# A six-sublayer decoder on one core: another table of turns for its two lanes, with the same instructions

## Chip, cores and metric

The kernel runs on one core of a Trainium2 chip. The metric is the device time of one execution in microseconds (us); the time of a kernel is the median of its runs. TensorE (PE) multiplies matrices, VectorE (DVE), ScalarE (ACT) and GpSimd (POOL) work on elements, and SyncE (SP) issues most of the transfers.

## The reference

Input x is 4 sequences of 512 tokens with 128 channels, and there is a context of 32 tokens for each sequence. Six sublayers follow each other, each as `x = layernorm(x + f(x))`:

```python
x = ln(x + mamba(x))                 # selective scan over 512 tokens, 256 channels, 16 states
x = ln(x + cross_attention(x, ctx))  # 16 heads of 64, inner layernorm, gate
x = ln(x + experts(x))               # shared FFN and 8 experts of 512, top 2 of 8
x = ln(x + window_attention(x))      # 16 heads of 8, causal window of 128, rotary
x = ln(x + cross_attention(x, ctx))  # 16 heads of 8
x = ln(x + two_local_layers(x))      # 8 heads of 64, window 64, then a gated FFN of 341, twice
```

All of it is float32 in the interface, and every sequence goes through all six in order.

## The kernel before

The four sequences go over the core in two lanes. Lane 0 takes sequences 0 and 1, one after the other, lane 1 takes 2 and 3; I call a lane's first sequence pass 1 and its second pass 2. Each lane has buffers of its own (names ending in `_0` and `_1`) and four of the eight PSUM banks, so the two lanes never share data. They do share the engines, and one engine executes its instructions strictly in program order, waits included. An instruction of lane 1 that must wait therefore holds back whatever of lane 0 stands behind it on that engine, and the other way round.

Each stage is written once for each engine, as a Python generator that yields at the places where the engine may be handed over (`mamba_vector`, `cross_tensor` and so on). For each engine `interleave` then merges the two lanes by the table `TURNS`: the first number says how many steps lane 0 takes, the next how many lane 1 takes, and so on in turn.

```python
lanes, done = (first, second), object()
for lane in lanes:
    next(lane)
last = [next(lanes[k % 2], done) for k, n in enumerate(turns) for _ in range(n)]
```

There is one list each for PE, ACT, DVE, POOL and SP. So the table alone decides the order of the instructions of one lane against those of the other on each engine. Within a lane the order is that of the generators.

The stages and the lines that the text below names:

- **Setup**, run once, in lane 1 ahead of its first stage. PE folds the context into the weights of the two cross attentions (L563, L567, L575, L584, L592, L597), DVE takes the results out of PSUM (L517, L524, L536, L538) and makes a rotary table (L552).
- **Mamba.** A preamble (projections L702, L706, L712, L719 and L726 on PE; the convolution L855 and L857 on DVE; the step size, L789 to L805 on ACT and L865 to L882 on DVE) and then the scan over 16 states. Each state takes on DVE one product L893 and two scans L901, on ACT two decays L822 and a copy L829, on POOL one product L930, on PE two broadcasts L738 and two sums L749. The decay of a lane lies in one PSUM bank: ACT writes it, the scan reads it, and only then can the next decay be written. After the 16th state come L907 (gating), L760 on PE, the residual L676 and two layernorms (L628 to L640).
- **Cross attention**: four tiles of 128 tokens. For each, PE L956, DVE L1023 and L1024, ACT L989, DVE L1014 and L1015, POOL L1038, PE L970, ACT L995, PE L962. Then the residual L678 and a layernorm (L609 to L618, with the root L652 on POOL).
- **Experts.** The shared FFN (PE L1064, L1094), routing on DVE (L1178 to L1241), a scatter of the tokens to DRAM by POOL, and then 15 blocks of 128 sorted tokens. L1105 transposes the sorted tokens, L1119 is the up and L1133 the down product of a block. The weights of a block are 512 KB, loaded by SP (L1921) into a ring of four buffers for each lane. Then a gather by POOL (L1286) and a layernorm.
- **Window attention**: PE L1459, L1466, L1441, then 14 units with PE L1325, L1330 (scores), DVE L1422, ACT L1385 and PE L1312.
- **Second cross attention and two local layers**: PE L1552, L1597 to L1629, ACT L1717, DVE L1771 to L1847, and the gated FFN (statistics PE L1640 and L1643, ACT L1735 and L1738, DVE L1842 to L1847; products PE L1650 and L1653, ACT L1744, DVE L1857; PE L1657 and L1665, DVE L1862).

Of the kernel before, what the change touches and what calls it, by code (L numbers as in the profile page):

```python
# [103 lines left out]
        4, 4, 1, 21, 2, 1, 1, 1, 1, 2, 1, 5, 1, 1, 1, 2, 3, 2, 3, 4, 3, 1, 5, 1, 1, 2, 2, 2, 1, 3, 3, 3, 3, 3,  # L104
        2, 1, 2, 2, 1, 3, 3, 3, 3, 5, 3, 3, 3, 3, 3, 3, 2, 3, 1, 3, 1, 5, 1, 1, 3, 1, 6, 1, 2, 4, 1, 1, 4, 3, 1,
        2, 2, 6, 1, 2, 3, 1, 4, 1, 4, 9, 2, 2, 14, 4, 2, 1, 1, 1, 1, 1, 5, 2, 2, 3, 2, 2, 4, 3, 1, 14, 1, 1, 1,
        1, 1, 1, 23, 1, 5, 1, 3, 1, 1, 2, 1, 1, 1, 1, 1, 1, 1, 4, 1, 1, 1, 5, 2, 2, 2, 1, 1, 1, 4, 1, 4, 3, 2,
        1, 1, 1, 2, 3, 3, 2, 3, 1, 1, 5, 5, 4, 2, 1, 3, 4, 1, 2, 2, 3, 2, 1, 1, 1, 1, 5, 3, 2, 1, 3, 3, 1, 2, 1,
        1, 3, 1, 2, 2, 3, 1, 1, 1, 1, 3, 6, 1, 5, 1, 4, 1, 3, 2, 2, 1, 2, 1, 1, 1, 1, 1, 1, 6, 1, 2, 3, 3, 2, 1,
        8, 1, 1, 1, 1, 3, 2, 1, 1, 1, 1, 6, 1, 1, 7, 7, 2, 2, 1, 1, 2, 3, 3, 1, 3, 1, 2, 2, 2, 4, 4, 7, 4, 1, 3,  # L110
        1, 2, 1, 2, 3, 4, 6, 4, 2, 2, 2, 1, 1, 3, 1, 2, 2, 4, 1, 2, 1, 3, 3, 1, 4, 3, 3, 2, 1, 2, 4, 1, 3, 3, 2,
        2, 3, 5, 8, 3, 1, 2, 5, 3, 1, 2, 1, 1, 2, 2, 3, 2, 2, 4, 6, 4, 1, 1, 1, 4, 2, 2, 4, 4, 4, 4, 2, 1, 2, 2,
        1, 3, 1, 2, 2, 4, 1, 2, 1, 3, 3, 1, 4, 3, 3, 7, 5, 5, 4, 2, 1, 3, 5, 2, 3, 3, 3, 3, 4, 3, 2, 1, 3, 2, 1,
        3, 7, 3, 3, 3, 4, 4, 2, 1, 2, 1, 1, 2, 2, 1, 1, 2, 3, 3, 2, 3, 1, 3, 1, 5, 1, 1, 3, 1, 6, 1, 1, 2, 1, 1,
        1, 2, 4, 3, 2, 1, 1, 7, 1, 2, 3, 1, 4, 1, 1, 1, 2, 2, 1, 6, 1, 2, 15, 3, 2, 2, 2, 1, 3, 1, 2, 1, 2, 3,
        1, 1, 1, 2, 4, 1, 1, 16, 1, 2, 1, 1, 22, 1, 2, 1, 1, 1, 3, 2, 1, 1, 2, 4, 1, 2, 1, 2, 1, 1, 1, 3, 2, 4,
        2, 1, 1, 2, 1, 2, 2, 1, 4, 3, 3, 2, 2, 1, 1, 3, 3, 1, 1, 2, 1, 1, 1, 2, 3, 2, 2, 3, 5, 2, 1, 2, 4, 1, 1,
# [2048 lines left out]
```

## Time and profile before

| | before |
|---|---|
| Median of 3 runs | 1492.87 us (1489.36 to 1494.64) |
| Time of the profiled execution | 1502.43 us |
| Its span, from the first to the last instruction | 1500.6 us |
| PE, DVE, ACT, POOL busy | 81%, 66%, 54%, 26% of the span |
| Mean granted clock of TensorE | 0.91 of full speed |

The profile is of one execution, which took 9.6 us longer than the median of the runs. "Busy" is the time in which an engine executed an instruction; "idle before" is how long it stood still ahead of one. A granted clock of 1.00 is 2.4 GHz and one of 0.50 is 1.2 GHz; numbers between are means over a stretch.

### The profile page before, as it was taken

Reading aid. Unit: us, or ns where it says so; the run is one execution under the profiler, and the core shown is the slowest. Engines: PE = TensorE matmul, PEld = TensorE weight load, DVE = VectorE, ACT = ScalarE, POOL = GpSimd, SP = SyncE. Lnnn points to the kernel's source line nnn. Section 1 sums busy time; section 2 is a strip of 40 time slices with the busy share of each in tenths; the row PEclk is TensorE's granted clock in tenths of the full one; section 3 lists DMA queues with packets and bytes.
Section 4 is the critical chain, followed back from the end, with each engine's and each line's share of the span. In section 5 each row is a group of like instructions: output and inputs, shape, how many; then the busy total and the mean of one; then the engine's idle time right before and its main releaser. Section 6 shows DMA issues by size and latency. Waiting matters only on the chain.

```text
span 1500.6 us, 23083 instructions
## 1 busy us (share of the span) xinstructions
PE 1210.9 (81%) x8416; PEld 773.4 (52%) x8416; DVE 988.3 (66%) x1914; ACT 813.1 (54%) x2170; POOL 393.6 (26%) x248
## 2 busy tenths in 40 slices
PE   5668768897799789889875776788879987888986
PEld 4313235786566446556531232468846654565563
DVE  5789976414555689459559999651265556984974
ACT  2365523263576367757637643225447734776873
POOL 0045732603000143023011666242220013311310
PEclk9878988899799999999987998779989988999998
DMA  8300000675000011001010000037710000000100
GB/s 304 129 0 1 0 1 0 197 251 158 6 2 2 1 43 30 1 8 30 7 28 0 1 0 1 0 115 238 226 34 1 2 1 8 22 16 8 29 9 15
DMA packets 42177, 72.20 MB, mean 48 GB/s; under 512 B 3793, under 2 KB 27473, under 8 KB 41810
## 3 DMA queue, kind: packets, MB, share of 16 engines
q1 hardware_dynamic: 40018, 66.53, 14.0%
q0 software_dynamic: 2048, 4.20, 0.9%
q8 instruction: 68, 1.11, 0.3%
q14 instruction: 43, 0.35, 0.1%
HBM read 51.19 MB, written 13.24 MB: 43 GB/s over the span
## 4 chain that ended last, share of the span: by engine, by line
PE 48%; DVE 25%; ACT 14%; issue 7%; DMA 3%; POOL 2%; SPq 0%; DVEq 0%; POOLq 0%; ACTq 0%
DVE scratch L901 5%; PE psum L1330 4%; PE psum L1552 3%; PE psum L1119 3%; DVE scratch L893 3%; PE psum L1312 3%; ACT scratch L1717 3%; ACT scratch L1385 3%; PE psum L749 3%; PE psum L1133 2%; PE psum L1441 2%; PE psum L1325 2%; PE psum L956 2%; PE psum L1597 2%; PE psum L1627 2%
## 5 line engine op out<-in xcount | busy, mean ns | idle before, releaser
L930 POOL TENSOR_TENSOR scratch<-scratch 128x1024 f32<-128x1024 f32 x64 | 151.9, 2384 | 141.0 <-DVE scratch L901 122.0
L652 POOL TENSOR_TENSOR small<-small,w_const 128x16 f32<-128x16 f32 x32 | 95.5, 2990 | 254.1 <-DVE small L1761 254.1
L901 DVE TENSOR_TENSOR_SCAN scratch<-psum,scratch 128x512 f32<-128x512 f32 x128 | 149.8, 1206 | 8.6 <-ACT psum L822 7.9
L749 PE MATMUL psum<-scratch,w_const 128*128 128x512 f32 x256 | 141.1, 681 | 14.6 <-POOL scratch L930 14.6
L652 POOL TENSOR_TENSOR rstd<-rstd,w_const 128x4 f32<-128x4 f32 x32 | 32.5, 1019 | 387.0 <-DVE rstd L614 379.2
L1385 ACT ACTIVATE scratch<-psum,mx 128x256 f32<-128x256 f32 (+1 forms) x256 | 111.1, 457 | 26.2 <-DVE mx L1422 25.5
L822 ACT ACTIVATE psum<-scratch,a_neg 128x512 f32<-128x512 f32 x128 | 88.0, 691 | 60.9 <-DVE scratch L901 58.7
L738 PE MATMUL psum<-scratch,cb 96*128 96x512 bf16 x128 | 50.8, 422 | 73.9 <-DVE scratch L893 65.7
L1422 DVE TENSOR_REDUCE mx<-psum 128x4 f32<-128x1024 f32 (+1 forms) x56 | 68.2, 1220 | 51.8 <-PE psum L1330 51.8
L1171 ACT ACTIVATE scratch<-psum,scratch 128x128 f32<-128x128 f32 x240 | 68.2, 372 | 60.5 <-PE psum L1119 60.5
L1552 PE MATMUL psum<-w_local,hT 128*128 128x512 f32 x192 | 96.0, 628 | 1.7 <-ACT hT L1534 1.7
L1717 ACT ACTIVATE scratch<-psum,mx 128x128 f32<-128x128 f32 x256 | 91.2, 404 | 10.6 <-DVE mx L1808 10.5
L1251 DVE COPY scratch<-psum 128x128 f32<-128x128 f32 x60 | 16.7, 289 | 116.8 <-PE psum L1133 116.7
L749 PEld LDWEIGHTS psum<-scratch,w_const 128*128 128x128 f32 x256 | 51.4, 214 | 68.6 <-issue 41.2
L1119 PE MATMUL psum<-scratch,expert_weights 128*128 128x128 f32 x480 | 67.6, 287 | 16.3 <-DMA expert_weights<-in_expert_weights 11.7
L738 PEld LDWEIGHTS psum<-scratch,cb 96*128 96x128 bf16 x128 | 13.0, 102 | 129.7 <-DVE scratch L893 96.6
L893 DVE TENSOR_TENSOR scratch<-scratch,psum 128x1024 f32<-128x1024 f32 x64 | 75.9, 1200 | 6.0 <-PE psum L738 5.7
L1312 PE MATMUL psum<-w_const,scratch 128*128 128x128 f32 x448 | 69.5, 292 | 5.2 <-ACT scratch L1371 3.3
L1119 PEld LDWEIGHTS psum<-scratch,expert_weights 128*128 128x128 f32 x480 | 60.6, 199 | 20.7 <-DMA expert_weights<-in_expert_weights 14.8
L829 ACT ACTIVATE scratch<-psum 128x512 f32<-128x512 f32 x64 | 38.0, 594 | 55.6 <-PE psum L738 55.5
L1330 PE MATMUL psum<-scratch 32*128 32x256 f32 (+1 forms) x512 | 67.6, 390 | 0.0
L1312 PEld LDWEIGHTS psum<-w_const,scratch 128*128 128x128 f32 x448 | 52.2, 148 | 27.8 <-issue 23.2
(274 smaller groups left out, 3060.0 us busy)
## 6 DMA issues: line engine op xcount, KB each, us to landing
expert_weights<-in_expert_weights SPq DMA_DIRECT2D x61, 512.0 KB, 4.8
scratch<-scratch SPq DMA_DIRECT2D x48, 128.0 KB, 2.3
folded_products<-expert_weights SPq DMA_DIRECT2D x8, 512.0 KB, 2.6
folded<-folded_products SPq DMA_DIRECT2D x8, 512.0 KB, 3.8
w_local<-in_local SPq DMA_DIRECT2D x1, 3122.0 KB
sorted_y<-scratch SPq DMA_DIRECT2D x12, 256.0 KB, 5.3
scratch<-sorted_x SPq DMA_DIRECT2D x4, 704.0 KB, 6.6
scratch<-in_cross SPq DMA_DIRECT2D x1, 2624.5 KB, 12.7
```

Of the source, the lines that this page charges most:

```text
L652: t.eng.tensor_tensor(v, v, W("const", "neg_half").to_broadcast([P, v.shape[1]]), ALU.pow).then_inc(t.s[done], 1)
L749: ins = pe.matmul(sum_banks[c], ident, t.m.hC[:, 2 * ((n - 1) % 2) + c, :], start=(n == 1), stop=(n == NS))
L822: act.activation(t.ps["dA"], t.m.delta[:, c, :], ACT.Exp, scale=a_neg[:, c, n:n + 1])\
L893: dve.tensor_tensor(t.m.dBu[n % 2], t.m.du[:, :, :], bank, ALU.mult).then_inc(t.s["v_freed"], 1)
L901: dve.tensor_tensor_scan(t.m.hs[:, n % 2, c, :], t.ps["dA"], t.m.dBu[n % 2][:, c, :], 0.0, ALU.mult, ALU.add)\
L930: t.eng.tensor_tensor(t.m.hC[:, 2 * (n % 2):2 * (n % 2) + 2, :], t.m.hs[:, n % 2], C, ALU.mult)\
L1119: ins = pe.matmul(tok(bank, f), t.m.weights[b % BUFS][:, f * P:(f + 1) * P], tok(t.m.xsT, b), start=(f == 0), stop=(f == NF - 1), skip_gro ...
L1312: ins = pe.transpose(tok(bank, c), tok(t.m.wide_pr[:, n % 2, u, :], c), ident)
L1330: ins = pe.matmul(banks[u][:, a * nk * P:(a + 1) * nk * P], t.m.wide_qT[r:r + 32, g, j * P:(j + 1) * P], t.m.wide_kT[r:r + 32, g, (j + 1 - ...
L1385: ins = act.activation(t.m.wide_pr[:, n % 2, u, z], bank[:, z], ACT.Exp, bias=t.m.mx2[:, c:c + 1], accum_out=t.m.sums[:, j % 2, h:h + 1])
L1552: pe.matmul(ring.open(), tok(t.m.hT, i), w_qkv[:, c * 512:(c + 1) * 512], start=True, stop=True).then_inc(t.s[sig], 1)
L1717: ins = act.activation(tok(t.m.pr[:, u, :], a), tok(bank, a), ACT.Exp, bias=t.m.mx2[:, c:c + 1], accum_out=t.m.sums2[:, c:c + 1])
```

## The change

Each of the five lists of `TURNS` is replaced by another. Nothing else differs: no generator, no buffer, no semaphore and no shape. Of the 76 lines of the table one stands here as it was and as it is, the start of PE's list; the numbers themselves say little to a reader.

```diff
     "pe": [
-        4, 4, 1, 21, 2, 1, 1, 1, 1, 2, 1, 5, 1, 1, 1, 2, 3, 2, 3, 4, 3, 1, 5, 1, 1, 2, 2, 2, 1, 3, 3, 3, 3, 3,
+        5, 9, 4, 7, 1, 10, 2, 3, 1, 1, 2, 2, 1, 1, 2, 1, 7, 1, 2, 3, 1, 1, 5, 2, 4, 2, 3, 1, 4, 1, 2, 1, 1, 3,
```

The new table is a line longer, so every line number of the code is one higher in the changed kernel (L712 becomes L713). What the lists do is seen in the order of the built programs. On DVE, ACT, PE, POOL and SP each lane executes the same instructions in the same order as before, and only their merging differs. ACT has one more kind of instruction that follows from the order: where two neighbours need functions from different tables, the compiler puts a table load between them. There are 45 of these in the program before and 51 after. Four of the added ones are in the first mamba, two in the first experts stage of lane 0 (around an exponential of lane 1's cross attention), one at the end of pass 1, and at the end of pass 2 there is one less.

PE near the start, before: lane 0's preamble (scratch_0, w_mamba) against the setup (scratch_1, expert_weights).

```order
L567 MATMUL psum<-scratch_1 128x128 x2
L575 MATMUL psum<-scratch_1 128x64 x8
L584 MATMUL psum<-scratch_1 64x128 x8
L575 MATMUL psum<-scratch_1 128x64 x8
L584 MATMUL psum<-scratch_1 64x128 x8
L575 MATMUL psum<-scratch_1 128x64 x8
L584 MATMUL psum<-scratch_1 64x128 x8
L575 MATMUL psum<-scratch_1 128x64 x8
L712 MATMUL psum<-scratch_0,w_mamba 8x512 x2
L719 MATMUL psum<-scratch_0,w_mamba 96x512 x2
```

The same place after:

```order
L703 MATMUL psum<-xT_0,w_mamba 128x512 x2
L707 MATMUL psum<-xT_0,w_mamba 128x512 x2
L564 MATMUL psum<-scratch_1 128x128 x9
L713 MATMUL psum<-scratch_0,w_mamba 8x512 x2
L720 MATMUL psum<-scratch_0,w_mamba 96x512 x2
L727 MATMUL psum<-scratch_0,w_mamba 128x512 x2
L564 MATMUL psum<-scratch_1 128x128 x7
L739 MATMUL psum<-scratch_0,cb 128x512
L568 MATMUL psum<-scratch_1 128x128 x2
L576 MATMUL psum<-scratch_1 128x64 x8
```

Lane 0's preamble stood behind seven groups of L575 and L584 and now stands ahead of all of them. DVE is alike: the last pair of L857 of lane 0 stood behind 16 of L517 and all 8 of L524, and stands behind one of L517 now; before lane 0's first L893 stood all of the setup, and 4 of the 16 instructions L536 and L538 stand there now. Lane 1's first stage starts on DVE (L844) after the first scan product of lane 0 before, and after six states of lane 0 now.

DVE where lane 1 ends its first mamba, before (y_0, mx_0 and sums_0 are lane 0, in its cross attention):

```order
L893 TENSOR_TENSOR scratch_1<-scratch_1,psum 128x1024
L633 TENSOR_SCALAR rstd2_0<-mv_0 128x4
L635 TENSOR_SCALAR rstd_0<-mv_0 128x4
L901 SCALAR_TENSOR_TENSOR scratch_1<-psum,scratch_1 128x512 x2
L640 TENSOR_SCALAR scratch_0<-y_0,mv_0,rstd2_0 128x128 x4
L640 TENSOR_SCALAR x_0<-y_0,mv_0,rstd_0 128x128 x4
L1023 TENSOR_REDUCE mx_0<-psum 128x16
L907 TENSOR_TENSOR scratch_1<-psum,scratch_1 128x512 x2
```

The same place after:

```order
L894 TENSOR_TENSOR scratch_1<-scratch_1,psum 128x1024
L902 SCALAR_TENSOR_TENSOR scratch_1<-psum,scratch_1 128x512
L679 TENSOR_TENSOR y_0<-psum,x_0 128x512
L902 SCALAR_TENSOR_TENSOR scratch_1<-psum,scratch_1 128x512
L610 BN_STATS rowstat_0<-y_0 128x6 x4
L613 BN_AGGR mv_0<-rowstat_0 128x2 x4
L615 TENSOR_SCALAR rstd_0<-mv_0 128x4
L619 TENSOR_SCALAR x_0<-y_0,mv_0,rstd_0 128x128 x4
L908 TENSOR_TENSOR scratch_1<-psum,scratch_1 128x512 x2
```

The end of lane 1's mamba stood next to the start of lane 0's cross attention and now stands behind its end: lane 0 leads by a stage more. In the experts stage this lead is given back. Before lane 1's first transpose of sorted tokens (L1105) PE had 6 blocks of lane 0 finished before and has 8 now, and after it follow 24 blocks of both lanes before and 22 now. Lane 0's window attention, which started on PE ahead of lane 1's last two blocks, starts behind them all. From the second cross attention of pass 1 on, the two orders are close to each other, within a few instructions at most places.

PE at the very end of pass 2, before (the gated FFN of both lanes):

```order
L1569 MATMUL psum<-w_local,scratch_1 128x128 x4
L1650 MATMUL psum<-scratch_0,w_local 128x512
L1653 MATMUL psum<-scratch_0,w_local 128x512
L1650 MATMUL psum<-scratch_0,w_local 128x512
L663 MATMUL psum<-w_const,x_1 128x128 x4
L1653 MATMUL psum<-scratch_0,w_local 128x512
L1650 MATMUL psum<-scratch_0,w_local 85x512
L1640 MATMUL psum<-hT_1,w_const 128x512
L1653 MATMUL psum<-scratch_0,w_local 85x512
L1657 MATMUL psum<-w_rows 128x512
L1643 MATMUL psum<-scratch_1,w_const 128x512
L1665 MATMUL psum<-w_local,scratch_0 128x128 x12
```

The same place after:

```order
L1570 MATMUL psum<-w_local,scratch_1 128x128 x4
L1644 MATMUL psum<-scratch_0,w_const 128x512
L664 MATMUL psum<-w_const,x_1 128x128 x4
L1641 MATMUL psum<-hT_1,w_const 128x512
L1644 MATMUL psum<-scratch_1,w_const 128x512
L1651 MATMUL psum<-scratch_0,w_local 128x512
L1654 MATMUL psum<-scratch_0,w_local 128x512
L1651 MATMUL psum<-scratch_0,w_local 128x512
L1651 MATMUL psum<-scratch_1,w_local 128x512
L1654 MATMUL psum<-scratch_1,w_local 128x512
L1651 MATMUL psum<-scratch_1,w_local 128x512
L1654 MATMUL psum<-scratch_0,w_local 128x512
```

Lane 1's last transpose and statistics moved ahead of all of lane 0's gated products, and the two lanes' products alternate. At the end of pass 1 the move is another: there lane 0's twelve L1665 stood behind lane 1's first three gated products, and stand ahead of them now, and on ACT lane 0's last L1744 stood behind lane 1's L1738 and stands ahead of it.

## Rows read from the trace of the kernel before

**Rows 1.** Busy time of the engines, clock by slice, chain that ended last (page).

```profile
PE 1210.9 (81%) x8416; PEld 773.4 (52%) x8416; DVE 988.3 (66%) x1914; ACT 813.1 (54%) x2170; POOL 393.6 (26%) x248
...
PEclk9878988899799999999987998779989988999998
...
PE 48%; DVE 25%; ACT 14%; issue 7%; DMA 3%; POOL 2%; SPq 0%; DVEq 0%; POOLq 0%; ACTq 0%
```

**Rows 2.** Stretches: window, length, busy of PE PEld DVE ACT POOL, PEclk, DMA share, GB/s.

```profile
62.80:190.80 128.00, 94.15 (x203) 33.94 (x203) 116.35 (x113) 73.67 (x112) 71.03 (x31) 0.86 0.02 7
...
305.00:366.00 61.00, 51.38 (x410) 48.18 (x408) 13.00 (x62) 29.50 (x100) 8.78 (x9) 0.94 0.65 210
366.00:386.00 20.00, 13.07 (x81) 8.90 (x81) 12.74 (x47) 8.71 (x26) 8.84 (x9) 0.84 0.23 64
386.00:414.00 28.00, 24.62 (x154) 15.55 (x153) 14.44 (x53) 15.20 (x53) 0.00 (x0) 0.81 0.00 1
414.00:500.00 86.00, 76.85 (x828) 50.76 (x826) 50.32 (x84) 58.59 (x224) 1.01 (x1) 1.00 0.01 2
```

**Rows 3.** Timeline of the start: start us, us, engine, line, [idle before <-releaser].

```profile
23.32 4.85 DVE L517 TENSOR_TENSOR scratch<-psum,w_const 128x256 f32<-128x256 f32 x13
28.17 4.87 DVE L524 TENSOR_TENSOR expert_weights<-psum,w_const 128x512 f32<-128x512 f32 x8
...
34.98 1.34 ACT L789 ACTIVATE scratch<-scratch,w_mamba 128x512 f32<-128x512 f32 x2 [13.61 <-DVE scratch L857]
...
39.02 1.88 PE L712 MATMUL psum<-scratch,w_mamba 128*8 128x512 f32 x4
...
58.68 2.76 DVE L552 TENSOR_TENSOR tab<-scratch 128x256 f32<-128x256 f32 x8
...
62.80 1.22 DVE L893 TENSOR_TENSOR scratch<-scratch,psum 128x1024 f32<-128x1024 f32 x1
```

**Rows 4.** Timeline of DVE: both L907, lane 0's L618 and lane 1's L1233.

```profile
190.77 1.26 DVE L907 TENSOR_TENSOR scratch<-psum,scratch 128x512 f32<-128x512 f32 x2
...
215.01 1.28 DVE L907 TENSOR_TENSOR scratch<-psum,scratch 128x512 f32<-128x512 f32 x2
...
245.07 1.11 DVE L618 TENSOR_SCALAR x<-y,mv,rstd 128x128 f32<-128x128 f32 x4
...
281.42 0.17 DVE L1233 TENSOR_SCALAR scratch<-scratch 128x15 uint32<-128x15 f32 x1
```

**Rows 5.** The records of L1133 alone, 8 for a block; columns as in rows 2.

```profile
305.00:366.00 61.00, 25.37 (x194) 23.17 (x192) 0.94 0.65 210
```

**Rows 6.** Timeline of PE: lane 1's first L1105, lane 0's last L1133, both window starts (L663).

```profile
304.98 0.60 PE L1105 MATMUL psum<-w_const,scratch 128*128 128x128 f32 x4
...
336.51 2.05 PE L1133 MATMUL psum<-expert_weights,scratch 128*128 128x128 f32 x16 [0.54 <-ACT scratch L1171]
...
358.71 1.12 PE L663 MATMUL psum<-w_const,x 128*128 128x128 f32 x4 [2.22 <-DVE x L618]
...
385.58 1.06 PE L663 MATMUL psum<-w_const,x 128*128 128x128 f32 x4
```

**Rows 7.** Timeline of ACT and PE at the end of pass 1.

```profile
753.15 0.63 ACT L1738 ACTIVATE scratch<-scratch 128x512 f32<-128x512 f32 x1
753.80 1.28 ACT L1744 ACT_TABLE_LOAD   x1
755.09 0.68 ACT L1744 ACTIVATE scratch<-psum,w_local 85x512 f32<-85x512 f32 x1
...
759.51 2.84 PE L1665 MATMUL psum<-w_local,scratch 128*128 128x128 f32 x24
```

**Rows 8.** Timeline of PE at the end of pass 2.

```profile
1469.72 0.60 PE L663 MATMUL psum<-w_const,x 128*128 128x128 f32 x4
...
1475.69 2.84 PE L1665 MATMUL psum<-w_local,scratch 128*128 128x128 f32 x24
1480.36 1.12 PE L1650 MATMUL psum<-scratch,w_local 128*128 128x512 f32 x2 [1.82 <-DVE scratch L1847]
```

131 rows, old and new, of the table TURNS are left out of this document.

## Prediction

> **What bounds the kernel now.** I began with the busy times. PE is busy for 81% of the span, and 48% of the chain that ended last are PE's, 25% DVE's, 14% ACT's [rows 1]. No engine is the bound throughout, so I went on by stretches of time. In 62.8 to 190.8, the first mamba, DVE is busy for 116.35 of 128 us, 91%, and PE for 94.15, at a clock of 0.86: DVE bounds. In 305 to 366, the expert blocks of both lanes, PE has 51.38 of 61. In 366 to 386, where lane 0 starts its window and lane 1 waits for its gather, no engine reaches 14 of 20 us, and the 28 us behind it, with PE at 24.62, run at a clock of 0.81. From 414 to 500 PE has 76.85 of 86 at a clock of 1.00 [rows 2]. A table of turns takes no work away. It can gain only where the bounding engine stands idle (1.0 − 0.91 of the mamba, some 20 us of PE between 305 and 414: 9.6 + 6.9 + 3.4), where PE's clock is low, and at the start, at the pass boundary and at the end, where one lane is alone.
>
> **The start.** The engines obey program order, so I looked in the timeline for work of the setup ahead of lane 0's preamble. ACT's L789 at 34.98 waited 13.61 us for a result of DVE L857, and this L857 stood behind thirteen L517 (4.85 us) and eight L524 (4.87). PE's L712 follows at 39.02 [rows 3]. With both groups behind it L857 ends 9.7 us earlier; the two or three L536 and L538 that also stood ahead of it are some 0.6 more. So L789 comes at about 24.7. From L789 to lane 0's first L893 at 62.80 are 27.8 us. In that piece DVE now also has the 9.7 us of L517 and L524, but no longer twelve of L536 and L538 (about 0.65 each, 7.8), the eight L552 (2.76 [rows 3]) and 1.3 us of small ones, together 11.9. 27.8 + 9.7 − 11.9 = 25.6, and the first L893 comes at 24.7 + 25.6 = 50.3, 12.5 us earlier.
>
> **Lane 0's mamba and cross attention.** Between lane 0's first L893 and its L907 stand, by the order of instructions, 11.9 us of setup more and six L893 and twelve L901 of lane 1 fewer, at 1.2 us each (the L893 of [rows 3] took 1.22): 21.6 less. 116.35 + 11.9 − 21.6 = 106.6 us of DVE work, at the density of now, 0.909, take 117.3. Lane 0's L907 comes at 50.3 + 117.3 = 167.6 instead of 190.77 [rows 4], 23 earlier. Here I chose the old density; six states of lane 0 alone could be less dense, with nothing of the other lane to fill the wait from scan to decay. L907 to the last L618 of lane 0's cross attention took 54.3 us (245.07 − 190.77 [rows 4]), which gives 221.9.
>
> **Lane 1.** What was moved ahead of it is its price. Its L907 stood next to lane 0's first L1023 and stands behind lane 0's L618 now: about 223.5 instead of 215.01, 8.5 later. From there to the end of its routing, L1233 at 281.42, were 66.4 us [rows 4]; less of lane 0 stands in that way, which I put at 4 us, an estimate from the few cross instructions of 0.7 to 1.3 us that are no longer there. L1233 comes at about 286, and the first L1105, 23.6 us later as now (304.98 − 281.42, [rows 4, 6]), at 309.5, 4.5 later. Queued behind that L1105 on PE are all further blocks of lane 0. They would wait with it.
>
> **The expert blocks.** 194 records of L1133 in 61 us [rows 5] are 24 blocks, 2.54 us each. After lane 1's first L1105 there are 22 blocks now, since two more of lane 0 stand ahead of it: 309.5 + 22 × 2.54 = 365.4, against 366. The 4.5 us are paid for. Lane 1's window start, at 385.58 [rows 6], hangs on its last block and stays within 1 us. Lane 0's last L1133 was at 336.51 and its window's first transpose 22.2 later, at 358.71 [rows 6]. Now this L663 stands behind lane 1's blocks, at 366 to 367. In the old order PE had blocks to do until 366 anyway, so most of these 8 us are no loss. I put the stretch up to 500 at +2, with −8 and +10 as bounds. The −8 would need the stretch of 28 us to lose its idle 3.4 us and its low clock (0.19 of 24.62 is 4.7). The +10 is what remains if lane 0's window is late by 8 us with nothing in its place, and 2 us at low clock.
>
> **From 500 on.** The orders differ by few instructions until the end of pass 1. There lane 0's last L1744 (755.09) stood behind a table load of 1.28 and an L1738 of 0.63 of lane 1, and its L1665 at 759.51 behind lane 1's gated products [rows 7]. Lane 0 begins pass 2 with what L1665 gives: −2, between 0 (DVE has lane 1's statistics to do in the meantime) and −4. At the end of pass 2, PE's transpose L663 of lane 1 at 1469.72 stood behind lane 0's gated products, and PE idled 1.82 us before lane 1's L1650 at 1480.36, behind the 24 L1665 of lane 0 [rows 8]. With L663 ahead of all products it comes some 3 us earlier, and products of lane 0 fill the wait: −4, between 0 and −6.
>
> **Table loads.** Six more on ACT, each 1.28 us; the activation behind one starts 0.01 us after its end (753.80 + 1.28, 755.09 [rows 7]). ACT is busy 73.67 of 128 us in the mamba, and 29.50 of 61 with the experts [rows 2]. I put them at 0, since DVE's and PE's work hides them; without this cover, they are 7.7 us. The Trainium skill (ScalarE: Activation LUTs, What ACT_TABLE_LOAD costs) gives about 2.66 us for every switch, as it adds a drain to the load, by which six would be 16 us. The rows here show no such drain.
>
> **The sum.** +2 − 2 − 4 + 0 = −4 us, against the profiled execution (1502.43 us, 9.6 above the median), so 1498.4 for it and 1489 on the scale of the median, 1492.87. All that lane 0 gains in the first 220 us is given back in the experts stage, as the merged order makes the lanes meet there.
>
> **The rivals.** A difference below 0.3%, 4.5 us, can't be told from none here.
>
> *The lead is kept (1478).* Lane 0's blocks begin earlier, its weights arrive while lane 1 is still in its routing, and both lanes' blocks and windows fit into PE's gaps. Between 305 and 414 lie 19.9 us of idle PE and 4.7 of low clock [rows 2]; half of them, 11, come off besides my 4. For it speaks that the blocks take 2.54 us each where PE works 2.14 (51.38 / 24), against it that the DMA engines are busy for 0.65 of that time, and that lane 1 is behind.
>
> *Nothing changes (1493).* The first 23 us vanish and the ends are held by DVE, whose last statistics follow one another whatever PE does. For it speaks that DVE is next to PE in each end.
>
> *Lane 1 starves PE (1505).* Lane 1's L907 is tied to lane 0's L618. If scanning lane 0 alone is less dense, or its cross attention has waits of its own, and L618 comes at 234.5 instead of 222, L907 is at 236, 21 later than before, and lane 1's first L1105 at 322. PE stands before it with lane 0's blocks queued behind. That is 12.5 us of wait beyond my sum, and then a run at a low clock: 8 us at 0.5 instead of 0.94 lose 3.5. −4 + 12.5 + 3.5 = +12. It decides the sign from where L618 is later than about 227 (5 us of wait and 3.5 of clock against the 4). In this kernel the clock was 0.86 where PE was busy 74% and 1.00 where it was busy 89% [rows 2]. By the Trainium skill (TensorE: Matmul & The Clock Gate, Part 1: The HAM clock gate) idle gaps bring the half clock back, so such a wait is paid for twice; the rows agree in direction.
>
> *Table loads on the path (1497).* Six loads of 1.28 us come off the ACT chain between scan and decay and before lane 0's expert activations: −4 + 7.7 = +4.
>
> **How the numbers follow.** The forecast has 0.42, of which 0.18 lie beyond −4.5; its own range is 1484 to 1494. The lead is kept 0.22, nothing changes 0.08, PE starves 0.20, table loads 0.08, half of that slower than the bound. Faster 0.18 + 0.22 = 0.40, within 0.24 + 0.08 + 0.04 = 0.36, slower 0.20 + 0.04 = 0.24. The range reaches from a little below the kept lead, 1476, to just over the starved case, 1506.
>
> **What the profile would show.** L789 near 25 and lane 0's first L893 near 50; lane 0's L907 near 168 and L618 near 222, lane 1's L907 right behind it; L1105 of lane 1 near 310 with little idle time ahead of it; the last block near 366, lane 1's window start near 385; the same stages as now from 500 on, less 2 us after 760 and 4 at the end. The prediction is wrong if PE idles for more than some us before lane 1's L1105 (slower), if the last block comes before 358 (the lead is kept), or if the second pass, which I hold for nearly unchanged, drifts by more than 3 us.

## The result, and the profile after

| | before | changed |
|---|---|---|
| Median, first chip | 1493.76 us (4 runs, 1489.36 to 1505.45) | 1473.69 us (4 runs, 1467.91 to 1480.25) |
| Ratio, first chip | | 0.9876 (95% interval 0.9841 to 0.9911) |
| Profiled execution: span, mean clock | 1500.6 us, 0.91 | 1478.5 us, 0.915 |

The change makes the kernel 1.24% faster, 18.5 us by the ratio and 20 by the two medians. I had forecast 4 us, inside the bound of what a measurement tells from none, and the measured time lies below my range. Two later timings of the changed kernel gave 0.9859 and 0.9865. The ratios leave out executions more than 1.5% above the fastest of the same kernel: four of the twelve of e5_start, and one of the kernel before.

Busy times, clock by slice and the chain that ended last, of the changed kernel's page (before: [rows 1]):

```profile
PE 1204.4 (81%) x8416; PEld 771.2 (52%) x8416; DVE 983.9 (67%) x1914; ACT 818.2 (55%) x2176; POOL 393.3 (27%) x248
...
PEclk9678999998799989999987999889979989999998
...
PE 46%; DVE 25%; ACT 15%; issue 7%; POOL 3%; DMA 3%; SPq 0%; DVEq 0%; POOLq 0%; ACTq 0%
```

Nothing in these sums says where 20 us went. The work is the same, and ACT has its six table loads more. The start and the front of the changed kernel, from its timeline (start us, us, engine, line; lines are one higher than before):

```profile
24.12 1.33 ACT L790 ACTIVATE scratch<-scratch,w_mamba 128x512 f32<-128x512 f32 x2 [2.69 <-DVE scratch L858]
25.89 1.88 PE L713 MATMUL psum<-scratch,w_mamba 128*8 128x512 f32 x4
47.95 1.21 DVE L894 TENSOR_TENSOR scratch<-scratch,psum 128x1024 f32<-128x1024 f32 x1
179.34 1.26 DVE L908 TENSOR_TENSOR scratch<-psum,scratch 128x512 f32<-128x512 f32 x2
230.66 1.12 DVE L619 TENSOR_SCALAR x<-y,mv,rstd 128x128 f32<-128x128 f32 x4 [1.12 <-POOL rstd L653]
231.69 1.28 DVE L908 TENSOR_TENSOR scratch<-psum,scratch 128x512 f32<-128x512 f32 x2
288.36 0.18 DVE L1234 TENSOR_SCALAR scratch<-scratch 128x15 uint32<-128x15 f32 x1
307.47 0.60 PE L1106 MATMUL psum<-w_const,scratch 128*128 128x128 f32 x4
351.31 1.16 PE L1134 MATMUL psum<-expert_weights,scratch 128*128 128x128 f32 x8 [0.40 <-ACT scratch L1172]
355.56 1.12 PE L664 MATMUL psum<-w_const,x 128*128 128x128 f32 x4 [3.09 <-DVE x L619]
378.40 1.11 PE L664 MATMUL psum<-w_const,x 128*128 128x128 f32 x4
```

Against [rows 3, 4, 6]: L789 comes at 24.12 instead of 34.98 and the first L893 at 47.95 instead of 62.80, both as worked out. Lane 0's L907 is at 179.34, 12 us later than my 167.6, and yet the last block of the experts is done at 352.5 and not at 365. The same kernel's stretches (window, length, busy of PE, PEld, DVE, ACT, POOL, clock, DMA share, GB/s), to be held against [rows 2]:

```profile
48.00:179.30 131.30, 99.51 (x265) 44.74 (x265) 111.82 (x119) 66.77 (x103) 56.20 (x25) 0.79 0.09 36
307.80:354.00 46.20, 40.28 (x350) 39.17 (x348) 9.73 (x39) 25.61 (x88) 8.30 (x9) 1.00 0.76 228
354.00:384.00 30.00, 20.12 (x82) 13.19 (x82) 15.37 (x82) 9.47 (x26) 9.10 (x10) 0.62 0.15 42
384.00:414.00 30.00, 27.04 (x193) 17.33 (x194) 16.01 (x39) 18.86 (x80) 0.00 (x0) 0.87 0.00 1
```

The blocks are denser and finished sooner; the hole between blocks and windows, 30 us with PE at 20.12 and a clock of 0.62, is as large as before or larger, and only earlier. DVE in the first mamba is busy for 0.85 of the stretch in this execution, whose clock was low at the start, not for the 0.91 that I had carried over.

### The profile page after: what moved, and what is told of

Read it like the earlier page. It is cut to its first block, busy times and chain, and to the rows that moved or that the text cites. A ratio compares the mean times of both kernels' runs of the same rounds, so it can differ in the third digit from the quotient of the medians.

```text
span 1478.5 us, 23087 instructions
## 1 busy us (share of the span) xinstructions
PE 1204.4 (81%) x8416; PEld 771.2 (52%) x8416; DVE 983.9 (67%) x1914; ACT 818.2 (55%) x2176; POOL 393.3 (27%) x248
## 4 chain that ended last, share of the span: by engine, by line
PE 46%; DVE 25%; ACT 15%; issue 7%; POOL 3%; DMA 3%; SPq 0%; DVEq 0%; POOLq 0%; ACTq 0%
DVE scratch L902 6%; PE psum L1331 3%; ACT scratch L1718 3%; PE psum L1553 3%; DVE scratch L894 3%; ACT scratch L1386 3%; PE psum L1313 2%; PE psum L1120 2%; PE psum L1134 2%; PE psum L750 2%; PE psum L957 2%; PE psum L1326 2%; PE psum L1442 2%; PE psum L1349 1%; PE psum L664 1%
## 5 line engine op out<-in xcount | busy, mean ns | idle before, releaser
L1553 PE MATMUL psum<-w_local,hT 128*128 128x512 f32 x192 | 92.3, 611 | 1.6 <-ACT hT L1535 1.3
L739 PEld LDWEIGHTS psum<-scratch,cb 96*128 96x128 bf16 x128 | 13.3, 104 | 123.5 <-DVE scratch L894 88.1
L1134 PE MATMUL psum<-expert_weights,scratch 128*128 128x128 f32 x480 | 64.1, 280 | 0.8 <-ACT scratch L1172 0.4
```

Source lines behind the costliest of these rows:

```text
L1134: ins = pe.matmul(bank[:, 0:D], t.m.hid[:, k % 2, f, :], t.m.weights[k % BUFS][:, FF + f * P:FF + (f + 1) * P], start=(f == 0), stop=(f == ...
L1553: pe.matmul(ring.open(), tok(t.m.hT, i), w_qkv[:, c * 512:(c + 1) * 512], start=True, stop=True).then_inc(t.s[sig], 1)
```

## The experiments

Both tables run through common states: points at which on every engine both have executed the same steps of both lanes. At such a point one table can be followed by the other. I used five: at about 350 us (end of the expert blocks of pass 1), 500 us (end of its window), 770 us (pass boundary) and 975 us (end of the cross attention of pass 2), and for one run 550 us. A run with such a joined table changes the order in its stretch and nowhere else, and keeps the line numbers of before. All ratios are against the kernel before, timed in the same session on the same chip, since chips differ: the kernel before had medians of 1510.86, 1497.38, 1495.16 and 1495.04 us in the four sessions, of which the second and the fourth were on one chip.

### Which stretch holds the gain: e1_front, e2_locals, e3_second

The edits, each as one piece of the difference in order against before. e1_front, PE at the start (as in the changed kernel up to 500 us):

```diff
-L706 MATMUL psum<-xT,w_mamba 128x512
-L563 MATMUL psum<-scratch 128x128 x4
-L706 MATMUL psum<-xT,w_mamba 128x512
-L563 MATMUL psum<-scratch 128x128 x12
+L706 MATMUL psum<-xT,w_mamba 128x512 x2
+L563 MATMUL psum<-scratch 128x128 x9
+L712 MATMUL psum<-scratch,w_mamba 8x512 x2
```

e2_locals, PE behind the join at 500 us (one piece of many):

```diff
-L970 MATMUL psum<-w_const,scratch 128x128 x4
+L1552 MATMUL psum<-w_local,hT 128x512 x3
+L970 MATMUL psum<-w_const,scratch 128x128 x4
+L962 MATMUL psum<-folded,scratch 128x128 x4
```

e3_second, PE in the cross attention of pass 2, where the last sums L749 of lane 1's scan stood ahead of lane 0's scores L956:

```diff
-L749 MATMUL psum<-scratch,w_const 128x512 x2
 L951 MATMUL psum<-w_rows 128x512
 L956 MATMUL psum<-folded,xT 128x512
+L749 MATMUL psum<-scratch,w_const 128x512 x2
+L956 MATMUL psum<-folded,xT 128x512
```

> The new table up to the end of pass 1's window attention, the old one behind it. In the two profiles lane 1 ends this window at 515 before and 513 after, lane 0 at 494 and 498. Theory A (the gain comes mostly from the second pass, where the two tables differ only by swaps of 1 to 4 neighbours): this run gains 2 us, between 0 and 5, so 1491 on the scale where before is 1493, and the second half of its profile looks like before's. Theory B (the second pass only inherits an arrangement of the lanes from the first 500 us): this run has most of the 20 us, 1473 to 1480.

> The old table, but the new one from the second cross attention of pass 1 to the end of pass 1 (500 to 770 us). In the profiles lane 0 leaves this stretch 7.9 us earlier and lane 1 4.5 us earlier, of which 2 were there before it. Theory A: 3 to 6 us faster, and the second pass as long as before. Theory B, now with the pass boundary as the place that arranges the lanes: the 3 us of lead that lane 0 gains at the boundary make the scan of pass 2 denser, so 10 to 14 us faster. My prediction had -2 for this stretch.

> The old table up to the pass boundary at 770 us, the new one for all of pass 2. Theory A: 13 to 16 us faster, of which about 8 in the mamba, 4 in the cross attention, 3 in the experts and 2 to 4 in the last stage. Theory B: the same instructions with neighbours swapped are worth nothing, and only the end's 2 to 4 us are gained. My prediction had -4 for this stretch.

| run | ratio (95%) | in us |
|---|---|---|
| e1_front | 0.9932 (0.9904 to 0.9960) | −10.3 |
| e2_locals | 0.9987 (0.9961 to 1.0014) | −2.0, not told from none |
| e3_second | 0.9969 (0.9942 to 0.9995) | −4.7 |

The us are (1 − ratio) × 1510.86. Neither theory holds as it was put. The front has about half of the gain and not the 2 us that I had read from the two profiles, nor all of it. The second pass has about a quarter. The 12 to 15 us which the first pair of profiles showed in pass 2 were mostly the two executions and not the order.

### Do the stretches add up: a2_changed, a3_changed

The changed kernel itself (its diff is the change), in two more sessions on one chip.

> The changed kernel again, on the chip of the next three. The first 500 us alone gave 0.68%, the locals 0.13% and the second pass 0.31%, 1.12% together. Theory A (the stretches add up): 1.0 to 1.3% faster. Theory B (they help each other, since a lead won in one is used in the next): more than 1.4%. For the start: in the first profile of the changed kernel TensorE's clock was 0.50 from 34 to 64 us and lane 0's L907 came at 179.3; the same order in the run of the front had it at 1.00, and L907 at 170.6. If the clock there is chance, this profile has either.

> The changed kernel again on the same chip, to compare the run of this call with, and for the state of the clock at the start: 0.94 to 1.00 in 34 to 64 us goes with L907 of lane 0 at 170 to 173, 0.50 with 179 to 181. The time is 1.2 to 1.5% below before.

0.9859 (0.9836 to 0.9882) and 0.9865 (0.9840 to 0.9890). The three stretches give 0.68 + 0.13 + 0.31 = 1.12%; within the intervals they add up, and a gain of the stretches from each other is not shown. Nor is it excluded: 1.41% is at the edge of theory B.

### Where in the front: e6_to_experts, e5_start, e7_old_start

e6_to_experts follows the new table up to the end of the expert blocks at 350 us and the old one behind it. Up to there its edit is that of e1_front, of which this is another piece, on PE: lane 1's preamble (L712, L719, L726) stands among later states of lane 0, between more of its L738 and L749. Behind the join lane 0's L663 stands ahead of lane 1's last blocks, as before.

```diff
 L712 MATMUL psum<-scratch,w_mamba 8x512 x2
 L719 MATMUL psum<-scratch,w_mamba 96x512 x2
+L738 MATMUL psum<-scratch,cb 128x512
+L744 MATMUL psum<-scratch,w_const 128x512 x2
+L749 MATMUL psum<-scratch,w_const 128x512 x2
 L726 MATMUL psum<-scratch,w_mamba 128x512 x2
```

> The new table up to the end of the expert blocks of pass 1 (about 350 us), the old one behind it. Theory A (the lead of lane 0 pays in the experts stage, because its blocks start earlier and lane 1's last block comes 8 to 10 us earlier than before): 8 to 10 us faster, as with the whole front (0.68%). Theory B (the gain needs the new order of the window too, where lane 0's L663 is behind lane 1's blocks): less than 5 us faster. Both have lane 1's last L1133 at 348 to 352, since the order up to there is the same.

0.9934 (0.9907 to 0.9960), −9.9 us: the time of theory A. The new order of the window stage adds nothing that these intervals show; the gain is made before 350 us. But its reason failed, and so did what both theories had: lane 1's last L1133 ended at 359.9, not at 348 to 352, with two of its blocks behind the window start of lane 0 again. From lane 1's first L1105 to its last block (columns as in [rows 2]):

```profile
307.00:360.00 53.00, 44.24 (x366) 42.99 (x365) 12.00 (x58) 26.34 (x89) 8.67 (x9) 0.94 0.65 199
```

These are 53 us, where the first profile of the changed kernel has 45 (307.47 to 352.47), and the gain is that of e1_front all the same. So how early the last block ends does not by itself set the time. Lane 1's window start, its L663, comes at 380.7 here, and at 378.40 and 379.9 in the two profiles of the changed kernel with the same low clock at the start.

e5_start moves the preamble only. All of the setup is still ahead of lane 0's first L893 (DVE):

```diff
-L517 TENSOR_TENSOR scratch<-psum,w_const 128x4x64 x13
-L524 TENSOR_TENSOR expert_weights<-psum,w_const 128x512 x8
-L538 COPY expert_weights<-psum 128x512
+L517 TENSOR_TENSOR scratch<-psum,w_const 128x4x64
 L857 SCALAR_TENSOR_TENSOR scratch<-psum,w_mamba,scratch 128x509 x2
```

> The old table, but the start as in the changed kernel: lane 0's mamba preamble ahead of the setup (L712 behind no L575 or L584, the last L857 behind one L517), with all of the setup still ahead of lane 0's first L893, and lane 1 never later than before. If the preamble behind the setup is a cost by itself, lane 0's first L893 comes 4 to 8 us earlier than 62.8 (DVE was busy for only 39.08 of these 62.8 us), both lanes keep it and the kernel is 4 to 8 us faster. If the start is given back whatever follows (lane 1's own preamble or the experts' weights set the time), the first L893 is earlier and the end within 2 us of before.

1.0015 (0.9988 to 1.0042), and its executions are spread widely, from 1503.62 to 1535.65 us. Both readings had the first L893 earlier, and in the profiled execution it came later. From its timeline:

```profile
71.87 1.20 DVE L893 TENSOR_TENSOR scratch<-scratch,psum 128x1024 f32<-128x1024 f32 x1
```

71.87 against 62.80 [rows 3]. The setup, pushed behind the preamble, ran on PE at half clock in this execution (29.46 of 30 us busy from 34 to 64 us, at 0.54), and the scan stood behind it. Its four pairs of L575 and L584 took 22.0 us, 5.5 each; a pair takes 3.0 in a2_changed at full clock. An estimate from these: at full clock the first L893 would have come 10 us earlier, at about 62, as before. So moving the preamble ahead is no gain by itself. The new table also puts the setup behind the first states; a run with that move alone was not made.

e7_old_start is the counterpart: the setup as before, all ahead of the first L893, then lane 0 alone for its first states, then the new order (DVE, against before):

```diff
 L893 TENSOR_TENSOR scratch<-scratch,psum 128x1024
+L901 SCALAR_TENSOR_TENSOR scratch<-psum,scratch 128x512 x2
+L893 TENSOR_TENSOR scratch<-scratch,psum 128x1024
+L901 SCALAR_TENSOR_TENSOR scratch<-psum,scratch 128x512 x2
```

> The new table, but all of the setup ahead of lane 0's first L893 as in the old one; then lane 0 alone for its first states, then the new order. It takes the start's 12 us away and keeps the distance between the lanes. If the start is worth what it brings (L893 at 48 instead of 62), this run is 8 to 12 us slower than the changed kernel, so about as fast as before. If the distance of the lanes is what matters and the start by itself is worth little, as the run with the start alone says (1.0015), it stays within 4 us of the changed kernel, 0.8% faster than before or more.

0.9929 (0.9905 to 0.9953), with a2_changed at 0.9859 on the same chip: 0.70%, 10.5 us slower than the changed kernel, as the first reading says, though not "about as fast as before". In the new order the start is worth what it brings. The other 0.7% remain, of which 0.44 are the stretches behind 500 us (e2_locals, e3_second), so about 0.3%, 4 us, are left for the distance of the lanes alone, which these intervals do not tell from none.

### The second pass: e4_mamba2, e8_late

e4_mamba2 has the new order only from 770 to 975 us. One piece on DVE, where lane 1's L907 let lane 0's cross attention wait:

```diff
 L1023 TENSOR_REDUCE mx<-psum 128x16
+L1024 TENSOR_TENSOR scratch<-psum,mx 128x512
 L907 TENSOR_TENSOR scratch<-psum,scratch 128x512 x2
-L1024 TENSOR_TENSOR scratch<-psum,mx 128x512
```

e8_late has it only behind 975 us. A piece of it on PE, in the window of pass 2, where lane 1's first transpose stands one unit of lane 0 earlier:

```diff
 L1330 MATMUL psum<-scratch 128x128 x8
+L663 MATMUL psum<-w_const,x 128x128 x4
 L1325 MATMUL psum<-cb 128x512 x2
 L1330 MATMUL psum<-scratch 128x128 x8
-L663 MATMUL psum<-w_const,x 128x128 x4
```

> The old table, with the new one only in the mamba and the cross attention of pass 2. In the first two profiles this piece (775 to 990 us) was 12 us shorter with the new table. Theory A (the swaps of neighbours in the scan matter): 4 to 8 us faster, the whole gain of the run with the new second pass (0.31%). Theory B (the 12 us were the clock of those two executions, 0.85 against 0.90): within 2 us of before, and the 0.31% come from the end.

> The old table up to the end of the cross attention of pass 2, the new one for the experts, the window and the last stages of pass 2. The run with only the mamba and the cross attention of pass 2 gave 0.22% (interval 0.5 to -0.1), the whole second pass 0.31%. Theory A (both halves of the second pass count; the experts of lane 1 took 111 to 115 us with the new order and 118 with the old one on two of the three chips): 3 to 6 us faster. Theory B (only the mamba and the cross attention count): within 2 us of before. My prediction had -4 for the end alone.

e4_mamba2: 0.9978 (0.9948 to 1.0008), −3.3 us, not told from none. e8_late: 0.9974 (0.9951 to 0.9996), −3.9 us. Each is near the 4.7 us (0.8 to 8.8) of the whole pass, and the three intervals overlap; how the gain splits stays open. DVE's longest waits in the last part of mamba and cross attention of pass 2, first in the kernel before (937 to 990 us), then in a2_changed (921 to 968), show one thing that moved:

```profile
DVE mx L1023 <- PE psum L956: 9.3, 4, 5.2
DVE sums L1014 <- ACT scratch L989: 3.1, 5, 0.7
```

```profile
DVE mx L1024 <- PE psum L957: 4.2, 3, 2.4
DVE sums L1015 <- ACT scratch L990: 1.9, 3, 0.7
```

The columns are us in total, times, longest. These two profiles differ by 5.1 us in the first of these waits. But over all profiles (880 to 1010 us) it goes with the order: the six with the old order in this piece have 6.7 to 9.3 us, the nine with the new one 4.2 to 6.0. Where the front is the old one too, 6.7 (e2_locals) and 9.3 stand against 6.0 and 6.0 (e3_second, e4_mamba2); where it is the new one, 7.2 and 7.7 (e6_to_experts, e1_front) against 4.2 to 4.5. So about 3 us of the wait go with the order, which fits the 3.3 us of e4_mamba2.

The end is settled by the traces as well. Lane 1's L1786 is a place up to which DVE has done the same work in both orders (kernel before, then changed):

```profile
1403.46 1.21 DVE L1786 TENSOR_TENSOR scratch<-scratch,small 128x1024 f32<-128x1024 f32 x1
```

```profile
1381.03 1.21 DVE L1787 TENSOR_TENSOR scratch<-scratch,small 128x1024 f32<-128x1024 f32 x1
```

From there to the end of the span are 97.2 us before (1500.6 − 1403.46) and 97.4 changed (1478.5 − 1381.03). In the other profiles it is 97.2 with the old order (98.4 in e6_to_experts) and 97.4 with the new one (97.8 in e3_second). The new order of the gated FFN at the end of pass 2 gains nothing; what e8_late gains lies between 975 us and this place.

### The clock at the start

Six profiles have the start of the changed kernel word for word. From 34 to 64 us, a2_changed and then e6_to_experts:

```profile
34.00:64.00 30.00, 27.01 (x185) 19.85 (x186) 29.94 (x42) 12.08 (x15) 4.72 (x2) 0.94 0.23 93
```

```profile
34.00:64.00 30.00, 29.31 (x149) 24.56 (x148) 22.86 (x32) 7.52 (x9) 2.37 (x1) 0.50 0.16 66
```

| profile | clock 34 to 64 us | lane 0's L907 |
|---|---|---|
| a2_changed | 0.94 | 172.4 |
| e1_front | 1.00 | 170.6 |
| f3_old_window | 1.00 | 171.3 |
| changed, first | 0.50 | 179.3 |
| e6_to_experts | 0.50 | 179.0 |
| a3_changed | 0.52 | 181.1 |

It is one or the other, and at the low level (1.2 GHz) L907 comes about 8 us later. It shows in the time: the three profiled executions with the low level took 4.3 to 6.6 us more than the median of their kernel's runs, the three others 0.6 to 3.3 less. PE is busy nearly all the time in it, 29.31 of 30 us. In the 20 us ahead of it, 14 to 34 us, PE was busy for 17.00 us at a clock of 0.99 in the first profile and for 16.07 us at 0.91 in a2_changed. In both the clock then fell at about 34 us. In a2_changed it was 0.57 from 34 to 38 us, with PE busy for 4.00 of 4 us, and 1.00 from 38 on; in the first profile it stayed at 0.50, with PE busy for 23.31 of 24 us from 36 to 60. So idleness ahead of it does not tell the two apart. By the Trainium skill (TensorE: Matmul & The Clock Gate, Part 1: The HAM clock gate) idleness is what brings the half clock; the trace agrees for the idle time of f5_scan_first below, and not for this fall. In the profiles of the old start the clock is 0.80 to 0.91 in the same 30 us. Two kernels tried to take the scan out of the way of this.

f2_broadcast, PE, against the new table:

```diff
 L575 MATMUL psum<-scratch 128x64 x8
 L584 MATMUL psum<-scratch 64x128 x8
+L738 MATMUL psum<-scratch,cb 128x512
 L575 MATMUL psum<-scratch 128x64 x8
 L584 MATMUL psum<-scratch 64x128 x8
 L575 MATMUL psum<-scratch 128x64 x8
 L584 MATMUL psum<-scratch 64x128 x8
-L738 MATMUL psum<-scratch,cb 128x512 x2
+L738 MATMUL psum<-scratch,cb 128x512
```

f5_scan_first has both L738 there, and on DVE, against the new table:

```diff
 L893 TENSOR_TENSOR scratch<-scratch,psum 128x1024
+L901 SCALAR_TENSOR_TENSOR scratch<-psum,scratch 128x512 x2
+L893 TENSOR_TENSOR scratch<-scratch,psum 128x1024
 L538 COPY expert_weights<-psum 128x512
-L901 SCALAR_TENSOR_TENSOR scratch<-psum,scratch 128x512
 L536 TENSOR_SCALAR expert_weights<-psum,gate 128x512
 L538 COPY expert_weights<-psum 128x512
-L901 SCALAR_TENSOR_TENSOR scratch<-psum,scratch 128x512
-L893 TENSOR_TENSOR scratch<-scratch,psum 128x1024
```

> The new table, with PE's broadcast L738 of lane 0's second half state moved ahead of the last two of the four pairs of groups L575 and L584. Where the clock is 0.50 from 34 to 64 us (three of five profiles with this start) each pair of groups takes 5.6 us on PE and DVE waits for this broadcast; two pairs are 11 us. Theory A (the low clock costs because the scan is queued behind the setup on PE): up to 8 us off at the low clock, none at the full clock, so 3 to 5 us faster than the changed kernel in the median and L907 of lane 0 near 171 at either clock. Theory B (the setup's copies on DVE are the limit at the low clock): L907 stays near 179 at the low clock and the time is the changed kernel's.

> The new table with two edits at the start. PE: the second and third broadcast L738 of lane 0 stand behind two pairs of L575 and L584, with the last two pairs behind them. DVE: the two scans L901 of lane 0's first state and the L893 of its second stand ahead of the setup's copies L538, which stood between them. In the run with the edit on PE alone DVE still waited 4.01 and 2.85 us for PE's L575 at those copies, with the scans queued behind them. Theory A (at the low clock the scan loses its 8 us behind these copies): at a clock of 0.5 to 0.7 in 34 to 64 us lane 0's L907 comes at 171 to 175 instead of 179 to 181, and the time is 2 to 5 us below the changed kernel's. Theory B (the setup's work on PE at half clock is delayed and taken from the scan a little later, whatever stands first): L907 at 178 or later at the low clock, and no gain.

f2_broadcast: 0.9917 (0.9884 to 0.9950); f5_scan_first: 0.9927 (0.9902 to 0.9952). f5_scan_first is 0.6% slower than the changed kernel on the same chip (0.9865 for a3_changed, the intervals don't meet). For f2_broadcast there is only f3_old_window on its chip (0.9882 (0.9852 to 0.9912)), from which it is not told: no gain shows, and no loss either. Lane 0's L907 comes at 180.6 and 181.9. The timeline of PE in f5_scan_first shows a wait that neither theory had:

```profile
39.31 2.00 PE L575 MATMUL psum<-scratch 128*128 128x64 f32 x16
41.28 1.09 PE L584 MATMUL psum<-scratch 128*64 128x128 f32 x16
49.47 0.61 PE L738 MATMUL psum<-scratch,cb 96*128 96x512 bf16 x1 [7.09 <-DVE scratch L893]
50.76 0.61 PE L738 MATMUL psum<-scratch,cb 96*128 96x512 bf16 x1 [0.69 <-ACT scratch L829]
51.16 3.51 PE L575 MATMUL psum<-scratch 128*128 128x64 f32 x16
```

The second broadcast writes a bank that the first L893 must have read, and that L893 comes at 48.20. PE stands for 7.09 us with the groups of the setup queued behind, and starts again at half clock (0.50 from 49 to 57 us): L575 takes 3.51 us for 16 where it had taken 2.00. In the changed kernel the four pairs of groups fill just this wait. I had priced the broadcast's move by who waits for it, and not by what it waits for.

### The window of pass 1: f3_old_window

The new table, with the old order from 350 to 550 us. Lane 0's L663 stands ahead of lane 1's last two blocks again (PE, against the new table):

```diff
-L1119 MATMUL psum<-scratch,expert_weights 128x128 x4
+L663 MATMUL psum<-w_const,x 128x128 x4
+L1119 MATMUL psum<-scratch,expert_weights 128x128 x4
+L1459 MATMUL psum<-w_window,xT 128x128 x4
 L1133 MATMUL psum<-expert_weights,scratch 128x128 x8
-L663 MATMUL psum<-w_const,x 128x128 x4
-L1459 MATMUL psum<-w_window,xT 128x128 x4
```

> The new table, with the old order from the end of the expert blocks of pass 1 to the end of the second cross attention of pass 1 (350 to 550 us). In the profiles with the old order there lane 1 needs 127 to 135 us from the end of its experts to the end of its window and 31.7 for the cross attention behind it, with the new order 135 and 34. Theory A (the new order of this piece costs 3 to 8 us, and the lead pays in spite of it): 3 to 8 us faster than the changed kernel, so 1.6 to 1.9% faster than before. Theory B (a lane that comes earlier into the window waits there whatever the order): within 2 us of the changed kernel.

0.9882 (0.9852 to 0.9912), 1475.96 us: level with the changed kernel, theory B for the end time, though not for its reason. Lane 1 left the window at 500.7 and the cross attention at 532.3 (a2_changed: 504.8 and 538.8), and the local layers at 761.9 (760.0). So 4 us were won in the window and 6.5 by the end of the cross attention, and lost again in the local layers. With the old order of this piece the last block ends later (351.8, and 347.9 in a2_changed), and the time is the same. No version that I ran beats the changed kernel.

## Why the prediction was wrong

**The start was right.** L789 near 24.7 (24.1), first L893 at 50.3 (47.7 to 49.8 in the six profiles).

**The first mamba, mis-sized.** 117.3 us from the first L893 to L907; it took 122 to 123.5 at the full clock (e1_front 170.6 − 48.6, a2_changed 172.4 − 48.9) and 131 at the low one. The density was right at the full clock: DVE was busy for 0.91 of the stretch in e1_front:

```profile
48.60:170.60 122.00, 88.52 (x225) 35.07 (x225) 111.34 (x120) 67.36 (x103) 56.18 (x25) 0.87 0.10 39
```

The work was not: 111.3 to 111.8 us where I had 106.6, so the exchange of lane 1's states for setup took 5 us off DVE and not 9.7. The doubt that I had noted, six states of lane 0 alone, does not show at the full clock. One that I had not seen, the clock, comes on top in three of the six profiles, with 8 to 9 us.

**The step that failed: "all that lane 0 gains in the first 220 us is given back in the experts stage", the +2 for the front.** e1_front has −10.3 us there. e7_old_start, with the new order but the old start, is 10.5 us slower than the changed kernel: the 12 to 14 us by which the first L893 comes earlier are kept for the most part. Lane 1's window start shows it. I held it within 1 us of 385.58; it came at 371.6 to 372.7 in the three profiles at full clock and at 378.4 to 380.7 in the three at the low one, against 382.5 to 386.6 with the old order and 383.2 in e7_old_start. Two terms of my sum, which charged lane 1's delay in full, were too large:

- *Lane 1's routing.* Its L907 was at 225.7 in a2_changed (223.5 forecast). From there to L1233 I took 62 us of the old 66.4; it took 56.7 (282.4), as in the rows above (288.36 − 231.69). From L1233 to the first L1105 I kept 23.6 us; it took 19.2 (301.6 − 282.4; 19.1 in the rows above). Together 10 us. By the order of instructions, 71 of lane 0 stood on DVE between lane 1's L907 and its L1233, nearly all of its cross attention among them, and 46 stand there now; no run tried this alone. So at full clock lane 1's blocks began no later than before (301.6 and 304.98 [rows 6], 300 to 307 in the other profiles of the old order), although its L907 was 10 us later; at the low clock they began at 307.05 to 309.12.
- *The expert blocks.* I divided 61 us by 24 blocks and had 2.54 us each, 55.9 for 22. The busy rows of the kernel before, cut at 357 us, show what was in these 61 us:

```profile
305.00:357.00 52.00, 44.15 (x372) 41.97 (x370) 9.44 (x38) 27.76 (x95) 8.28 (x9) 0.99 0.73 232
357.00:366.00 9.00, 7.23 (x38) 6.21 (x38) 3.56 (x24) 1.74 (x5) 0.50 (x1) 0.68 0.24 81
```

The last 9 us hold 16 records of L1133, two blocks, and with them 2.2 us in which PE stood before lane 0's L663 and 3.9 us of L663 and the window products behind it, at a clock of 0.68. The blocks before them took 2.36 us each (52 us for 22). In a2_changed, 302 to 348 us:

```profile
302.00:348.00 46.00, 41.73 (x349) 40.61 (x347) 9.69 (x39) 25.60 (x88) 8.31 (x9) 0.96 0.77 229
```

22 blocks in 46 us, 2.09 each, PE busy for 91% instead of 85%. 22 × (2.54 − 2.09) = 10 us, and the four profiles with the new order there have 45.0 to 47.5 us. Some 6 of the 10 are no gain for the kernel: they are lane 0's window start and the wait ahead of it, which the old mean had in it and the new order has behind the blocks. e6_to_experts and f3_old_window put it back among the blocks, need 53 us for them, and no loss shows in their times. And e7_old_start has 22 blocks in 46.4 us too, with a front worth only some 4 us. So the denser blocks pay for lane 1's later L907, and most of the front's gain is the start's.

**Behind it.** a2_changed has its last block 17 us earlier than the profile of the kernel before (347.9 and 364.8), but the one execution took 3 us less and the other 9.6 us more than the median of its kernel. With the old order the last block ended at 357.8 to 366.2 in five profiles, mean 362.0; with the new one at 347.9 to 356.4 in four, mean 351.4. From there to the end of its window lane 1 took 147 to 157 us with the old order and 157 to 159 with the new one, so about 6 of the 10.6 us are given back, in the hole with the low clock (0.68 from 348 to 378 us in a2_changed). The rival "the lead is kept", with −15 for the whole kernel, was nearer than my sum (−18.5), though not by its reason: the low clock stretch of the window that I let it fill is still there.

**The locals and the pass boundary.** −2 forecast, −2.0 measured (−5.9 to +2.1), not told from none.

**The second pass, right in size by luck.** −4 forecast for the end alone, −4.7 (−8.8 to −0.8) measured for all of it. The end itself gained nothing (97.2 and 97.4 us from L1786 on). What is gained comes from the swaps that I held for nothing, some 3 us of it with the wait for L956.

**Table loads.** DVE waited 6.1 us for ACT's L822 in the first mamba of before (62 to 191 us), 5.9 in that of a2_changed and 9.9 in that of the first profile of the changed kernel, at the low clock, with the added loads in both. At full clock the loads do not show in this wait, which speaks for my 0. One of them in the changed kernel's timeline at the end of pass 1:

```profile
747.58 1.28 ACT L1745 ACT_TABLE_LOAD   x1
748.87 0.68 ACT L1745 ACTIVATE scratch<-psum,w_local 85x512 f32<-85x512 f32 x1
749.57 1.28 ACT L1739 ACT_TABLE_LOAD   x1
```

From the end of the activation (748.87 + 0.68 = 749.55) to the next load are 0.02 us, and from a load to its activation 0.01. The drain that the Trainium skill adds to each switch (ScalarE: Activation LUTs, What ACT_TABLE_LOAD costs) is not seen here. No run tried the loads alone.

**The other rivals.** PE did not starve: its idle time ahead of lane 1's first L1105 is none in the rows (1.2 us in e1_front). The deciding point that I gave (L618 later than 227) was passed in the low clock executions (230.66) without the 12 us of loss, because lane 1's routing and its way to the first L1105 were 10 us shorter.

In sum: +2, −2, −4 became −10.3, −2.0, −4.7, together −17.0.

## What to carry to other kernels

A mean time for each unit, taken over a stretch, carries whatever else stands in it: cut the stretch where the foreign work begins, before the mean is used for a new order. What a lane needs from one point to the next depends on how much of the other lane is in between; if the change takes the other lane out, that time shrinks, and it has to be worked out again rather than carried over. And an instruction that is pulled forward in an in-order queue should be priced by what it waits for, since all behind it waits too. To say where a small gain lies, join the two orders at common points and time the pieces, and compare a stretch over all profiles at hand: two single profiles put 15 us into the second pass, of which 4.7 were measured when it was timed by itself.

## What the runs showed of the hardware

With the same start, TensorE's clock was 0.50 to 0.52 for 30 us in three executions and 0.94 to 1.00 in three. PE was busy for 96 to 98% of the low stretch, and lane 0's L907 came about 8 us later behind it. The level had fallen at 34 us in a2_changed too and was back at 38. What decides it is not settled. After 7.09 us of idle PE in f5_scan_first, L575 took 3.51 us for 16 instead of 2.00. And the median of the kernel before was 1495.04 and 1497.38 us in two sessions on one chip and 1510.86 on another, a difference almost as large as what the change is worth.
